# Third layer of one quad in every unit, in place of both quads of a group in every second unit

## The reference, cut to what matters

```
x = x + conv_block(ln_over_channels(x))         # sign(), 3x3 conv, batch norm, clip
t = tokens(x);  n = layernorm(t)
w = softmax(mean_over_images(n) @ Wr + br)      # gate of each pixel, 8 experts
h = relu(bn1(n @ W1[e] + b1));  h = relu(bn2(h @ W2[e] + b2))
t = t + sum_e w[e] * (h @ Wo[e] + bo[e])
```

## Time and profile before

| | before |
|---|---|
| median of 3 runs | 1488.68 us (1487.44 to 1496.91) |
| the profiled execution, its own time | 1496.05 us |
| its span in the trace | 1493.9 us |
| TensorE matmul busy | 1398.6 us, 94% of the span, x11864 |
| VectorE busy | 976.9 us, 65% |
| ScalarE busy | 805.9 us, 54% |
| GpSimd busy | 427.1 us, 29% |

### The profile page before, as it was taken

One profiled execution on the slowest core, in us unless ns is written; L12 is line 12 of the kernel. 1 busy time (PEld: TensorE's weight loads), 2 busy tenths in 40 slices (PEclk: granted clock), 3 DMA queues, 4 the chain that ended last, 5 costly groups with the idle time before them and its releaser, 6 DMA issues. The chain is left out here.

```text
span 1493.9 us, 33196 instructions
## 1 busy us (share of the span) xinstructions
PE 1398.6 (94%) x11864; PEld 568.9 (38%) x11864; DVE 976.9 (65%) x1599; ACT 805.9 (54%) x1139; POOL 427.1 (29%) x362
## 2 busy tenths in 40 slices
PE   3999966899999999999999999999999999999998
PEld 2666632333333333333333333333333333333332
DVE  5888853666665666665676656567565667666655
ACT  3666655455555555555555555555555455555442
POOL 7000053323313323313323312332322332322330
PEclk9999977999999999999999999999999999999999
DMA  9999732233332234333233332233332134333121
GB/s 156 173 156 147 107 50 50 49 72 70 73 66 45 49 68 74 68 60 49 51 68 74 68 68 43 50 68 74 68 74 52 35 68 74 68 68 57 38 51 26
DMA packets 360592, 105.53 MB, mean 71 GB/s; under 512 B 352656, under 2 KB 352880, under 8 KB 360560
## 3 DMA queue, kind: packets, MB, share of 16 engines
q1 hardware_dynamic: 359296, 103.49, 39.8%
q0 software_dynamic: 1264, 1.61, 0.6%
HBM read 78.97 MB, written 26.09 MB: 70 GB/s over the span
## 5 line engine op out<-in xcount | busy, mean ns | idle before, releaser
L715 ACT ACTIVATE h<-ps,bias 128x896 f32<-128x896 f32 x448 | 451.6, 1008 | 449.7 <-PE ps L532 448.7
L883 DVE SCALAR_TENSOR_TENSOR v<-ps,negb,wb 128x448 f32<-128x448 f32 x896 | 570.9, 679 | 159.4 <-PE ps L558 159.3
L532 PE MATMUL ps<-xc,w 64*64 64x448 f32 x3584 | 436.9, 551 | 14.9 <-issue 8.8
L558 PE MATMUL ps<-h,w 64*64 64x448 f32 x3584 | 431.9, 545 | 0.9 <-ACT gconst L746 0.5
L571 PE MATMUL ps<-v,wo 128*64 128x448 f32 x1792 | 362.9, 545 | 0.3 <-DVE v L883 0.2
L449 POOL TENSOR_TENSOR o<-xin,gconst 128x448 f32<-128x448 f32 x112 | 124.9, 1136 | 486.1 <-ACT gconst L746 387.6
L893 DVE TENSOR_TENSOR o<-ps,o 128x448 f32<-128x448 f32 x112 | 69.8, 623 | 251.2 <-PE ps L571 251.2
L427 POOL TENSOR_TENSOR xc<-xc,spread 128x896 f32<-128x896 f32 x56 | 126.7, 2279 | 375.1 <-DMA spread<-rs_rows 375.0
L532 PEld LDWEIGHTS ps<-xc,w 64*64 64x64 f32 x3584 | 118.0, 132 | 279.2 <-issue 277.8
L558 PEld LDWEIGHTS ps<-h,w 64*64 64x64 f32 x3584 | 133.7, 132 | 223.7 <-issue 214.1
L571 PEld LDWEIGHTS ps<-v,wo 128*64 128x64 f32 x1792 | 127.3, 136 | 192.2 <-issue 190.6
(11 more groups left out here) (142 smaller groups left out, 741.2 us busy)
## 6 DMA issues: line engine op xcount, KB each, us to landing
xa<-in_x SPq DMA_DIRECT2D x64, 392.0 KB, 6.5
xin<-in_x SPq DMA_DIRECT2D x56, 448.0 KB, 6.0
spread<-rs_rows SPq DMA_DIRECT2D x112, 224.0 KB, 4.1
out<-o SPq DMA_DIRECT2D x224, 112.0 KB, 2.5
rs_rows<-rs SPq DMA_DIRECT2D x112, 3.5 KB
rows<-in_L_ffn_g POOLq DMA_DIRECT2D x2, 256.0 KB, 5.9
rows<-in_L_ffn_v POOLq DMA_DIRECT2D x2, 256.0 KB, 6.8
cwt<-in_L_conv_weight SPq DMA_DIRECT2D x2, 144.0 KB, 2.6
```

What stands on the lines that cost most here:

```text
L532: last = mm(ps[64 * two:64 * two + 64, bank + ab, 0:NG], w1[half, P * q + C * two:P * q + C * two + C], xc[half, s, g // 2, ab ^ (g % 2), ...
L558: last = mm(ps[64 * i:64 * i + 64, bank + low, 0:NG], w2[rows_, Q + QUADS * i, :], h[rows_, u % 2, i, ab, :], start=True, stop=True)
L715: A(h[:, u % 2, i], ps[:, bank:bank + 2, 0:NG], ACT.Relu, bias=bias[:, 0, q:q + 1]).then_inc(h_done[i], 1)
L883: last = V.scalar_tensor_tensor(out=v[:, u % 2, ab, d, :].rearrange("p (b w) -> p b w", w=W), in0=ps[:, bank + d, 0:NG].rearrange("p (b w) ...
```

## The change

`layer3` now takes a unit and does one quad. The group's first quad keeps the wait for `out_done`, each quad keeps the wait for both `v_done` of its unit, and accumulation in bank 6 starts and stops at the same quads as before. TensorE's `chunk` calls it in every unit for the unit before, in the same place (behind layer 1 with i = 0 and the preparation point), where it was called at every second unit for two.

```diff
-                def layer3(k, g):
-
-                    pe.wait_ge(out_done, G * k + g + 1)
-                    for Q in range(QUADS):
-                        u = QUADS * g + Q
-                        for ab in range(2):
-                            pe.wait_ge(v_done[ab], UNITS * k + u + 2)
-                        for d in range(2):
-                            for par in range(2):
-                                last = mm(ps[64 * par:64 * par + 64, 6, 0:NG], wo[:, 2 * Q + d, :], v[:, u % 2, par ^ (g % 2), d, :],
-                                          start=(Q == 0 and d == 0), stop=(Q == QUADS - 1 and d == 1))
-                        last.then_inc(l3_done, 1)
+                def layer3(k, u):
+
+                    g, Q = u // QUADS, u % QUADS
+                    if Q == 0:
+                        pe.wait_ge(out_done, G * k + g + 1)
+                    for ab in range(2):
+                        pe.wait_ge(v_done[ab], UNITS * k + u + 2)
+                    for d in range(2):
+                        for par in range(2):
+                            last = mm(ps[64 * par:64 * par + 64, 6, 0:NG], wo[:, 2 * Q + d, :], v[:, u % 2, par ^ (g % 2), d, :],
+                                      start=(Q == 0 and d == 0), stop=(Q == QUADS - 1 and d == 1))
+                    last.then_inc(l3_done, 1)
...
-                        if u and u % QUADS == 0:
-                            layer3(k, u // QUADS - 1)
-                        elif u == 0 and not first:
-                            layer3(k - 1, G - 1)
+                        if u:
+                            layer3(k, u - 1)
+                        elif not first:
+                            layer3(k - 1, UNITS - 1)
...
-                        layer3(k, G - 1)
+                        layer3(k, UNITS - 1)
```

## The result

The changed kernel takes **1744.45 us** (median of 4 runs, 1743.20 to 1749.91) against 1489.47 us before; the ratio is 1.171, 95% interval 1.166 to 1.176. The direction was right, the size was not: +255 us where +167 was forecast, and outside the range.

A forecast was written before the change was run, and what follows sets the result against it. TensorE was taken to set the pace; five units at 5.63 us plus 6.49, 6.13 and 9.35 made a chunk 50.12 instead of 44.16 us, times 28 = +167 us, so 1656 us for the median, range 1630 to 1685.

The forecast's parts named there:

- The new wait: Ahead of layer 3 at units with nothing else there, TensorE waits for the preceding unit's pair, standing 0.8 us.
- the loop of 5.63 us: Units 1, 2, 3, 5 and 7: a loop through TensorE and VectorE makes each unit 5.63 us long.
- the single block of 1.65: Layer 3 on TensorE: a block of one quad takes 1.65 us to the next layer 2.
- Units 6 and 0 stayed covered: Preparation blocks ahead of layer 3 hide the wait; unit 6 goes from 7.49 to 6.13 us, unit 0 from 10.86 to 9.35.
- My own sum: Units of one chunk added up: 44.16 us before, 50.12 after, +5.96 a chunk, times 28 = +167 us.
- a chunk of 44.16 us: The one profiled chunk of the expert part, taken as the length before for all 28 chunks.
- The rival of the switches: Layer 3: only the 112 more blocks cost, 0.34 us each, 38 us in all, giving 1527 us; chance 4%.
- within 0.4 us after it became idle: VectorE's pairs: each starts at most 0.4 us after VectorE became idle; used against the rival of the switches.
- VectorE sets this one, before as after ... 6.49 before, 6.49 after: Unit 4: VectorE's pair, three x1 additions and add_out set its length, unchanged at 6.49 us.
- the 3.57 us of three additions: Unit 4 on VectorE: the three x1 after the pair at 713.92 take 3.57 us, within the unit's 6.49.
- a rival at 4%: TensorE's granted clock falls with the idle time; at 1.2 GHz for good over 2600 us, otherwise something between; chance 4%.
- The bounds: Start after the pair: 6 us; single block's 0.20 at nothing: 28 us less; add_out in unit 2's loop: +17 us.

The follow-up runs named there:

- wait alone, additions at unit 3: Kernel before with TensorE waiting for v_done[1] at every unit, no block moved or split, and the three x1 additions at unit 3 instead of 4: 1608.12 us (1.079).
- the changed kernel, additions at unit 3: Changed kernel with VectorE's three x1 additions at unit 3 instead of unit 4: 1620.45 us (1.087).
- four fillers: Changed kernel with four extra unread matmuls of 448 columns on TensorE ahead of the first layer 1 of unit 5: 1703.20 us (1.138).
- the first kernel with layer 3 two units late: Changed kernel with layer 3 in unit u taking the quad of unit u-2 instead of u-1, and add_out one unit later: 1649.30 us (1.107).
- holding GpSimd: Changed kernel with GpSimd beginning its feature sums only when VectorE's three x1 additions of the chunk are done: 1623.66 us (1.089).
- the kernel with the wait alone: Kernel before with TensorE waiting for v_done[1] of the unit before at every unit, no block moved or split: 1653.91 us (1.112).

## Why the prediction was wrong, by its own steps

The loss of 255 us, taken apart by neighbouring kernels. The last two rows are 77 and 48 by the ratios to the kernel before that ran beside each, and the third holds whatever the fillers cost themselves.

| step | kernels | us |
|---|---|---|
| the wait for `v` at every unit | before to wait alone, additions at unit 3 | +118 |
| blocks split and moved | from there to the changed kernel, additions at unit 3 | +12 |
| additions beside GpSimd, unit 4 | from there to four fillers | +83 |
| half clock behind the gap | four fillers to the changed kernel | +41 |

**The new wait, the loop of 5.63 us, the single block of 1.65: right.** 5.63 and 1.66 were measured. Units 6 and 0 stayed covered. The wait and the split together are 131 us. My own sum, with 28 x (6.49 - 5.63) = 24 us for unit 4 taken out, is 143. It was made against a chunk of 44.16 us; the distances between one `inv` and the next were 43.8 to 47.6 us in the kernel before, 44.66 in the mean, both without the first, and 28 x 0.50 = 14 us less make it 129. The wait alone is nine tenths of this. The rival of the switches (38 us; the prediction calls it the second, it is its first) was priced too dear: the split measured 12 us beside the wait, and 16 to 28 without it. One reading in it was also wrong: VectorE does not start every pair within 0.4 us after it became idle, the pair at 745.39 has 1.20.

**"VectorE sets this one, before as after ... 6.49 before, 6.49 after": the step that failed.** The failed step put unit 4 at 6.49 us. Measured were 8.5 us in the mean, and unit 5, put at 5.63, took 7.3 by the half clock behind it. I carried the 3.57 us of three additions over as a fixed duration. It was no property of them: one of the three had met GpSimd's multiplication (716.11 in the trace before), and 3.57 is two of 0.61 and one of 2.50, less their overlap. I should have asked who ran beside them, and what shifts if the units in front get longer. Nor did VectorE set unit 4 in the kernel before. In 12 of its chunks the additions met no GpSimd work, `add_out` then waited for TensorE, and unit 4 was the same 6.50 us (here 676.02 - 669.52):

```profile
669.52 1.28 DVE L883 SCALAR_TENSOR_TENSOR v<-ps,negb,wb 128x448 f32<-128x448 f32 x2 [0.23 <-PE ps L558]
670.71 1.69 DVE L903 SCALAR_TENSOR_TENSOR xin<-t,xin 128x448 f32<-128x448 f32 x3
673.67 0.62 DVE L893 TENSOR_TENSOR o<-ps,o 128x448 f32<-128x448 f32 x1 [1.27 <-PE ps L571]
...
676.02 1.27 DVE L883 SCALAR_TENSOR_TENSOR v<-ps,negb,wb 128x448 f32<-128x448 f32 x2 [0.23 <-PE ps L558]
```

With 3.57 us the additions just fitted, and with 5.46 us the unit took 8.3. So 6.49 was wrong for the changed kernel in both directions: 5.63 with quick additions (measured, with them at unit 3), 8.5 with those it got.

The change moved the two against each other from both sides. The additions follow the `inv` of unit 2 by two units, formerly 715.11 - 705.60 = 9.5 us, now 11.3 (two units of 5.63). GpSimd's multiplication followed the same `inv` by 716.11 - 705.60 = 10.5 us, now by 806.57 - 798.09 = 8.5. GpSimd starts after two transfers behind `inv`, and these don't follow the units; they are even shorter now (from the rows of the root to GpSimd 806.57 - 799.82 = 6.75 us against 716.11 - 707.33 = 8.78), probably since the large load of x is over when they begin:

```profile
793.33 2.33 SPq L284 DMA_DIRECT2D xin<-in_x  x2
...
799.82 1.12 SPq L295 DMA_DIRECT2D rs_rows<-rs  x4
801.88 2.42 SPq L299 DMA_DIRECT2D spread<-rs_rows  x4
```

Before, the load was issued at 703.29, 4.0 us ahead of the root's rows, and the spreading started 4.2 us behind these; now the load is 6.5 us ahead and the spreading starts after 2.1 us; in the first kernel with layer 3 two units late it was 2.2 us ahead and 6.0 us. The three agree, but that the load makes the difference is argued from them and not tried by itself: why the additions and GpSimd met stays in part open. What was tried is that the overlap costs the time, by moving the additions and by holding GpSimd.

**The clock: a rival at 4%, with the wrong shape.** I weighed whether many gaps of 0.8 us would lower it (they don't: 0.988 with all of them) or all would be at half speed. I didn't ask what a single gap of 3 us would do, because I had no such gap in the sum. The two errors are one: without the slow additions there is no such gap, and without it no half clock (0.988 with the additions at unit 3). In the trace of before the chunk at 1148.80 already showed the chain whole: 5.48 us of additions, a gap of 2.06 us on TensorE, clock 0.96.

**The bounds.** Those I took into the range were bounds of terms I had thought of. The duration of 3.57 us had its own spread in the trace of before, 611 to 2527 ns for one addition with a median of 618, where the page gives the mean of 938; with all three at the upper end, 7.5 instead of 3.57, unit 4 alone would have given up to 110 us more. A row whose mean is far from its median should have been a bound.

## What to carry to other kernels

A block put directly behind the producer of its newest input exposes that producer's whole latency, and old work in front of it is what hid it: before work is spread more evenly, look at what it covered. When a change lengthens some stages of a pipeline and not others, everything with a length of its own (transfers and what follows them) slides against the stages; check what it then runs beside, above all vector instructions with two SBUF inputs against GpSimd (0.61 us became up to 2.5 here). And read a mean beside its smallest and largest value before it goes into a sum.

## What the runs showed of the hardware

- A VectorE addition with two SBUF operands (128x448) took 0.61 us alone and up to 2.5 us beside GpSimd instructions of 1.4 to 2.5 us; it ended about 0.5 us after the one it met. VectorE instructions that read PSUM and one SBUF operand were not slowed (0.61 to 0.68 us).
- The granted clock stayed at 1.00 through five waits of 0.8 us a chunk. In the changed kernel it fell to 1.2 GHz at every one of the 26 gaps of TensorE of 2.9 to 3.8 us, at a price of 41 to 48 us in all. With layer 3 two units late it fell at 19 of 25 gaps of 3.0 to 4.2 us. Gaps of 1.8 to 2.2 us did both: in the kernel with the wait alone, two gaps of 2.06 us left the clock at 1.00 behind one (1131.06) and at 0.68 behind the other (978.88). Filling the gap with matmuls nobody read kept it at 2.4 GHz.
- With 36 more matmuls per chunk in the loop's body, TensorE stood two times, mostly 1.6 to 2.2 us, at the jump of the loop (every second chunk). What it waited for there the profile does not show.
- Splitting 112 blocks of 128x64 matmuls out between blocks of 64x64 cost 12 us beside the wait and 16 to 28 us without it, 0.1 to 0.25 us for each block more.
